# A fused state-space convolution and quantised FFN: down's loads, sums, mask, conversion, bank and skip-term moved

## The reference

```
mask = arange(512) < length[:, None];  u_m = x * mask
K = 2 * real(einsum(Cs, exp(dtA * arange(512))))      # one row of taps per head
y = (causal_conv(u_m, K) + u_m * D) * mask
xq    = int4_quant(y)                                 # scale from mean |y| of the row
w_eff = clip(round(w / mean|w|), -1, 1) * mean|w| * s # for w_gate, w_up, w_down
gate  = relu(xq @ w_gate_eff.T) ** 2;  up = xq @ w_up_eff.T
inter = int8_quant(up * gate)                         # scale from max |.| of the row
out   = x + inter @ w_down_eff.T
```

## Time and profile before

| | us |
|---|---|
| median of three runs | 210.07 |
| the profiled execution | 210.21 |
| its span (first to last instruction) | 208.0 |
| TensorE busy | 176.7 |
| VectorE busy | 166.5 |
| ScalarE busy | 114.2 |
| TensorE idle at 69.67, at 80.68, at 192.34 and at 198.39 | 1.46, 0.96, 0.66, 1.23 |

### The profile page before, as it was taken

How to read it: one execution, slowest core, us unless ns; L and a number is a source line. 1 busy time by engine, 2 the same in 40 slices (tenths; PEclk the granted TensorE clock), 3 DMA queues, 4 the chain that set the end, 5 groups by cost and what they waited for, 6 DMA issues and landing times.

```text
span 208.0 us, 3457 instructions
## 1 busy us (share of the span) xinstructions
PE 176.7 (85%) x1127; PEld 95.1 (46%) x1143; DVE 166.5 (80%) x456; ACT 114.2 (55%) x188; POOL 11.7 (6%) x31
## 2 busy tenths in 40 slices
PE   1011799799999798999999999999999999998973
PEld 1001697555554253455454545444545454543442
DVE  6999778759997686797979788878888787879871
ACT  2277957799817345364554637281919182735630
POOL 5035501100001000000000000000000000000000
PEclk9999999999999999999999999999999999999998
DMA  2999839149999399868596678696786979634524
GB/s 88 378 385 327 287 109 315 66 134 267 204 161 214 76 225 195 209 167 203 130 240 196 153 217 156 130 219 205 147 225 138 230 107 224 171 71 116 117 65 101
DMA packets 50784, 38.31 MB, mean 184 GB/s; under 512 B 37024, under 2 KB 37392, under 8 KB 50768
## 3 DMA queue, kind: packets, MB, share of 16 engines
q1 hardware_dynamic: 49968, 36.57, 71.6%
q10 hardware_dynamic: 416, 1.47, 2.1%
q0 software_dynamic: 384, 0.06, 0.2%
HBM read 25.27 MB, written 4.28 MB: 142 GB/s over the span
## 4 chain that ended last, share of the span: by engine, by line
PE 56%; DVE 16%; DMA 10%; ACT 9%; issue 5%; SPq 3%; DVEq 0%; ACTq 0%
PE down_ps L630 14%; PE conv_ps L500 12%; PE gate_ps L583 12%; PE up_ps L588 10%; DMA it_int<-inter_q 5%; DMA q_int<-y_i 4%; PE tr_act_ps L490 2%; ACT g L739 2%; ACT int_up L669 2%; DVE y L1012 1%; ACT y_i L705 1%; ACT int_gate L682 1%; PE tr_dve_ps L557 1%; ACT int_down L675 1%; DVE inter L1097 1%
## 5 line engine op out<-in xcount | busy, mean ns | idle before, releaser
L697 ACT ACTIVATE y_abs<-y 128x512 bf16<-128x512 f32 x16 | 10.1, 629 | 65.4 <-DVE y L1012 65.4
L588 PE MATMUL up_ps<-up_t,q_t 128*128 128x416 bf16 (+2 forms) x192 | 45.0, 357 | 0.0
L583 PE MATMUL gate_ps<-gate_t,q_t 128*128 128x416 bf16 (+2 forms) x177 | 41.9, 356 | 2.1 <-DVE q_t L1032 1.2
L630 PE MATMUL down_ps<-down_t,i_t 128*128 128x512 bf16 (+1 forms) x164 | 37.9, 379 | 3.8 <-DVE i_t L1138 3.6
L1097 DVE SCALAR_TENSOR_TENSOR inter<-up_ps,gu_scale,g 128x416 f32<-128x416 f32 (+2 forms) x48 | 33.2, 692 | 7.6 <-issue 5.2
L500 PE MATMUL conv_ps<-toep,x_t 128*64 128x512 f32 (+3 forms) x256 | 38.0, 439 | 0.2 <-ACT x_t L693 0.2
L739 ACT ACTIVATE g<-gate_ps,gu_scale 128x416 f32<-128x416 f32 (+2 forms) x48 | 30.3, 631 | 5.0 <-PE gate_ps L583 4.9
L1101 DVE TENSOR_REDUCE imax<-inter 128x1 f32<-128x416 f32 (+2 forms) x48 | 30.3, 631 | 1.6
L742 ACT ACTIVATE g<-g 128x416 f32<-128x416 f32 (+2 forms) x48 | 28.1, 586 | 1.5
L500 PEld LDWEIGHTS conv_ps<-toep,x_t 128*64 128x64 f32 x256 | 17.0, 136 | 23.1 <-issue 20.3
L588 PEld LDWEIGHTS up_ps<-up_t,q_t 128*128 128x128 bf16 x192 | 18.8, 98 | 18.4
(11 more groups left out here) (180 smaller groups left out, 161.6 us busy)
## 6 DMA issues: line engine op xcount, KB each, us to landing
toep<-k_back SPq DMA_DIRECT2D x16, 512.0 KB, 4.9
x_in<-in_x_dram SPq DMA_DIRECT2D x32, 128.0 KB, 3.0
x_res<-in_x_dram SPq DMA_DIRECT2D x32, 128.0 KB, 4.1
out_dram<-o_sb SPq DMA_DIRECT2D x30, 128.0 KB, 2.4
raw_gate<-in_L_ffn_w_gate_dram SPq DMA_DIRECT2D x1, 1536.0 KB, 7.0
raw_up<-in_L_ffn_w_up_dram SPq DMA_DIRECT2D x1, 1536.0 KB, 13.4
raw_down<-in_L_ffn_w_down_dram ACTq DMA_DIRECT2D x1, 1376.0 KB, 7.0
raw_down<-in_L_ffn_w_down_dram SPq DMA_DIRECT2D x1, 1376.0 KB, 8.7
```

Of the source, the lines that this page charges most:

```text
L583: mm = pe.matmul(gate_ps[bank][:, 0:cn], q_t[p][:, i, :], gate_t[:, i, c0:c0 + cn], start=(i == 0), stop=(i == KB - 1))
L588: mm = pe.matmul(up_ps[bank][:, 0:cn], q_t[p][:, i, :], up_t[:, i, c0:c0 + cn], start=(i == 0), stop=(i == KB - 1))
L630: mm = pe.matmul(down_ps[:], i_t[0:r, c, :], down_t[0:r, c, :], start=(c == 0), stop=(c == IB - 1))
```

## The change

Seven edits:

1. **Loads of down.** Both halves of `raw_down` are issued by SP's queue behind the Toeplitz tiles of tiles 0 and 1; the first half was issued by ScalarE's queue after ScalarE's second sum of up. Tile 2's `x` is issued right behind them, ahead of the wait for parts 1 and 2.
2. **Sums.** `down_sum(0)` on VectorE moves from before `y_mask(0)` to behind `q_copy(0)`, where `down_sum(2)` stands.
3. **Taps.** Parts 1 and 2 change places: part 1 is now the first 8 heads of group 1, part 2 the last 12 heads of group 0.
4. **Skip term.** The four loads of `d_tail` are issued by GpSimd ahead of its arithmetic instead of behind it.
5. **x kept.** Six `x` buffers (two of them in the space of `raw_up`) replace two `x_in` and two `x_res`; `add_out` reads the tile that `xt` read, and the 32 loads of `x_res` go. `oscale` gets a third buffer.
6. **Mask and bank.** In iteration 1 `y_mask(3)` goes ahead of `down_copy(0)`. down of tile 0 writes `tr_dve_ps` instead of `down_ps`.
7. **Conversion and output.** In iteration 2 the conversion of `i_t` moves from behind `gated(1)` and `add_out(0)` to ahead of `gated(1)`; `add_out(0)` goes behind `y_mask(4)`. The stores of tiles 0 and 1 are both issued in iteration 3.

```diff
-        x_in = [sb(f"x_in{p}", [P, L]) for p in range(2)]
-        x_res = [sb(f"x_res{p}", [P, L]) for p in range(2)]
+        x_in = [sb(f"x_in{i}", [P, L]) for i in range(4)] + [raw[1][:, i, :] for i in range(2)]
+        NX = len(x_in)
...
-        K_PARTS = [(0, 0, K_EARLY, 0, tr_dve_ps), (0, K_EARLY, HG, 32, tr_dve_ps),
-                   (1, 0, HG // 2, 64, tr_dve_ps), (1, HG // 2, HG, 0, down_ps)]
+        K_PARTS = [(0, 0, K_EARLY, 0, tr_dve_ps), (1, 0, HG // 2, 32, tr_dve_ps),
+                   (0, K_EARLY, HG, 64, tr_dve_ps), (1, HG // 2, HG, 0, down_ps)]
...
             load_toep(1, 1)
-            s = weight_part(2, 1)
-            sp.dma_start(raw[2][s], w_down.rearrange("(c p) i -> p c i", p=P)[s]).then_inc(w_loaded[2][1], 16)
+            for i in range(2):
+                s = weight_part(2, i)
+                sp.dma_start(raw[2][s], w_down.rearrange("(c p) i -> p c i", p=P)[s]).then_inc(w_loaded[2][i], 16)
+            load_x(2)
...
-                elif k >= 2:
-                    sp.wait_ge(out_ready, m - 1)
-                    for half in range(2):
-                        sp.dma_start(in_dram(out, m - 2, half), o_sb[p][half_rows(half), :]).then_inc(stored[p], 16)
+                elif k >= 3:
+                    for n in range(0 if k == 3 else m - 2, m - 1):
+                        sp.wait_ge(out_ready, n + 1)
+                        for half in range(2):
+                            sp.dma_start(in_dram(out, n, half), o_sb[n % 2][half_rows(half), :]
+                                         ).then_inc(stored[n % 2], 16)
...
-                if k is None or k < T:
-                    for half in range(2):
-                        sp.dma_start(x_res[p][half_rows(half), :], in_dram(x, m, half)).then_inc(res_loaded[p], 16)
...
-                wait(pe, out_ready, m - 1)
+                elif k == 2:
+                    pe.wait_ge(k_ready, 4)
+                else:
+                    pe.wait_ge(out_ready, m - 1)
...
-            down_sum(0)
             y_mask(0)
             y_scale(0, 0, step)
             weight_copy(10)
             k_copy(2)
             q_copy(0, 0)
+            down_sum(0)
             down_sum(2)
...
-                if k in (1, 2, T - 1):
+                if k in (1, T - 1):
                     gated(1)
-                if k == 2:
-                    add_out(0, down_ps, slice(0, L), 1)
...
                 if k == 1:
+                    y_mask(3)
                     down_copy(0)
-                    y_mask(3)
                     k_copy(3)
                 if k < T - 2 and k != 1:
                     y_mask(m + 2)
+                if k == 2:
+                    add_out(0, tr_dve_ps, slice(0, L), 1)
```

More of the change, by code:

```diff
@@ L164, in adaln_ffn @@
         iscale = sb("iscale", [P, 1])
-        oscale = [sb(f"oscale{p}", [P, 1]) for p in range(2)]
+        oscale = [sb(f"oscale{i}", [P, 1]) for i in range(3)]
         inter_q = sb("inter_q", [P, IB * P], I16)
@@ L180, in adaln_ffn @@
         w_loaded = [[sem(f"w_loaded{m}{i}") for i in range(3)] for m in range(3)]
-        x_loaded = [sem(f"x_loaded{p}") for p in range(2)]
-        res_loaded = [sem(f"res_loaded{p}") for p in range(2)]
+        x_loaded = [sem(f"x_loaded{i}") for i in range(NX)]
         toep_loaded = [sem(f"toep_loaded{p}") for p in range(2)]
@@ L310, in _, with load_x @@
                 sp.dma_start(dst, src).then_inc(par_loaded, 16)
-            def load_x(tile, p):
+            def load_x(tile):
+                b = tile % NX
+                if tile == 4:
+                    sp.wait_ge(w_rounded[1][0], 1)
                 for half in range(2):
-                    sp.dma_start(x_in[p][half_rows(half), :], in_dram(x, tile, half)).then_inc(x_loaded[p], 16)
+                    sp.dma_start(x_in[b][half_rows(half), :], in_dram(x, tile, half)).then_inc(x_loaded[b], 16)
             def load_inner(m, w):
@@ L326, in _ @@
             load_inner(1, w_up)
-            load_x(0, 0)
-            load_x(1, 1)
+            load_x(0)
+            load_x(1)
             sp.wait_ge(zeros_ready, 1)
@@ L358, in load_ahead @@
                     sp.wait_ge(k_stored[3], 16)
-                sp.wait_ge(xt_turned, n - 1)
-                load_x(n, p)
+                if n > 2:
+                    load_x(n)
                 sp.wait_ge(conv_done, n - 1)
@@ L421, in _ @@
             nc.gpsimd.memset(w_int[2][:, :, I:IB * P], 0).then_inc(pads_ready, 1)
+            pool.wait_ge(zeros_ready, 2)
+            for g, h0, h1, row, bank in K_PARTS:
+                last = row + JA - 1
+                pool.dma_start(d_tail[last:last + 1, h0:h1, JB - 1],
+                               Dskip[g * HG + h0:g * HG + h1].rearrange("(a h) -> a h", a=1),
+                               allow_slow_non_contiguous=True).then_inc(d_loaded, 16)
             steps_done = [0]
@@ L444, in _ @@
             tt(cs[:], cs[:], both(inv_a2[:, 2:3]), ALU.mult).then_inc(cs_ready, 1)
[L446 to L449, removed]
-                               Dskip[g * HG + h0:g * HG + h1].rearrange("(a h) -> a h", a=1),
-                               allow_slow_non_contiguous=True).then_inc(d_loaded, 16)
             pool.wait_ge(w_loaded[1][2], 32)
@@ L486, in xt @@
             def xt(n, j, p):
-                pe.wait_ge(x_loaded[p], 32 * (j + 1))
+                b = n % NX
+                pe.wait_ge(x_loaded[b], 32 * (n // NX + 1))
                 wait(pe, xt_copied, n)
                 for i in range(KB):
-                    mm = pe.transpose(tr_act_ps[:, i * P:(i + 1) * P], x_in[p][:, i * P:(i + 1) * P], ident[:])
+                    mm = pe.transpose(tr_act_ps[:, i * P:(i + 1) * P], x_in[b][:, i * P:(i + 1) * P], ident[:])
                 mm.then_inc(xt_turned, 1)
@@ L626, in down @@
                     pe.wait_ge(down_copied, 2)
-                wait(pe, out_ready, m - 1)
+                elif k == 2:
+                    pe.wait_ge(k_ready, 4)
+                else:
+                    pe.wait_ge(out_ready, m - 1)
                 for c in range(IB):
                     r = P if c < IB - 1 else IR
-                    mm = pe.matmul(down_ps[:], i_t[0:r, c, :], down_t[0:r, c, :],
+                    mm = pe.matmul(down_bank(m - 1)[:], i_t[0:r, c, :], down_t[0:r, c, :],
                                    start=(c == 0), stop=(c == IB - 1))
@@ L643, in body @@
                     if k == 2:
-                        pe.wait_ge(k_ready, 4)
                         down(1, 1)
@@ L1107, in add_out @@
                     dve.wait_ge(down_done, done)
-                    dve.wait_ge(res_loaded[q], 32 * (n // 2 + 1))
+                    dve.wait_ge(x_loaded[n % NX], 32 * (n // NX + 1))
                     wait(dve, stored[q], 32 * (n // 2))
                     v.scalar_tensor_tensor(out=o_sb[q][:, cols], in0=bank[:, 0:cols.stop - cols.start],
-                                           scalar=oscale[q][:], in1=x_res[q][:, cols],
+                                           scalar=oscale[n % 3][:], in1=x_in[n % NX][:, cols],
                                            op0=ALU.mult, op1=ALU.add).then_inc(out_ready, 1)
@@ L1146, in body @@
                         add_out(T - 1, bank, cols, T + h)
-                if k < T - 1 and k not in (1, 2):
+                if k < T - 1 and k != 1:
                     gated(1)
```

6 lines of the change are left out of this document (3 added, 3 removed).

## The result

Four runs of the changed kernel gave 206.90 to 207.23 us, median **207.14 us**; four of the kernel before, run beside them, gave a median of 210.32 us. The ratio is 0.985, with a 95% interval of 0.981 to 0.989: about 3.2 us faster. The profiled execution took 207.19 us with a span of 205.0, so that the two traces differ by 3.0 us.

The account below looks back on a forecast made before the run. TensorE's waits at the start and before down in iterations 2 and 3, behind VectorE and SP's queue, were taken as the places to gain; 0.3 + 1.6 + 1.1 + 0.3 = 3.3 us off 210.07 gives 206.8, range 206.0 to 207.7.

Parts of the forecast that it names:

- the forecast case: Whole launch: 206.8 us on the median's scale, own range 206.0 to 207.7, chance 0.60.
- Iteration 2: TensorE's 1.46 us wait for the conversion before down goes, with the pipe's refilling: 1.6 us, ends nothing and 1.7.
- The 0.15 for the pipe: TensorE in the loop's iteration 2: refilling of the pipe after the wait before down goes, about 0.15 us.
- Mask of tile 3 ahead of `down_copy(0)`: VectorE in iteration 1: same work in another order, worth nothing; at most 0.75 us lost if the copy comes late.
- Iteration 3: q's transposition on SP's queue issued some 5 us earlier, so the conversion's DMA lands in time: 1.1 us.
- Iterations 4 to 15: Loop's rest: 32 loads of 128 KB go, helping only tile 15's wait for q: 0.3 us, ends nothing and 0.66.
- The start: Before the loop's second iteration: what VectorE's list carries on of earlier taps, mask and products: 0.3 us, ends nothing and 0.75.
- Down's loads: SP's queue at the start: second half lands at 41.3 at the latest, wanted at 41.0, costing up to 0.3 us.
- Rival D: Start: down's second half lands far too late, each us after 41.0 costing one; 210.8 us, reaching 213; chance 0.04.
- Rival A: Start gives gain back: slow TensorE rate past conv(0), or late tap store delaying conv(2) 1.5 us; 208.3 or 207.3; chance 0.15.
- Rival B: One wait stays before down in iteration 2 or 3, 1.1 to 1.6 us missing: 207.9 to 208.4; chance 0.09.
- the rule of turns between the queues: DMA engines alternate packets between queues, so GpSimd's part 2 tap store would pass the backlog and its 1.5 us price vanish.

Follow-up runs that it names:

- The start's part alone: Kernel before with only edits 1 to 4 (loads of down, sums, taps, skip term), its loop as before; 209.69 us, ratio 0.999.
- Conversion back: Changed kernel with the conversion of iteration 2 behind `gated(1)` again, `add_out(0)` still behind the mask of tile 4; 206.75 us, ratio 0.985.
- conversion and mask back: Changed kernel with iteration 2's conversion behind `gated(1)` again and the mask of tile 3 behind `down_copy(0)` again; 208.30 us, ratio 0.994.

## Why the prediction was right, and where it was not

207.14 us against the forecast 206.8, inside its range, and faster as the forecast case said. Its steps:

- *Iteration 2*, 1.6 booked, 1.83 measured: right, but 0.13 above its upper end of 1.7, which took the extra down at its whole 2.55 us; it stretched the iteration by only 12.25 - 9.87 = 2.38. The 0.15 for the pipe is borne out: a down that had not waited started 0.16 us before the recorded end of the matmuls ahead of it (68.11 against 67.35 + 0.92). Within the term the causes were put wrong. "Mask of tile 3 ahead of `down_copy(0)`" was booked at nothing and the conversion's own move taken as the cause. Conversion back costs 0.06 us, conversion and mask back 1.07, so that with the mask early the conversion's own move was worth nothing, and the mask's place was worth 1 us once the conversion was late.
- *Iteration 3*, 1.1 booked, 1.13 measured: right, and its cause, q's place behind the stores, is shown for 0.74 of it by the run that puts them back. For q of tile 4, behind four stores, VectorE waited 0.76 us at 81.20 and TensorE not at all; with the same four stores that wait was 0.22 to 0.38 us or none in the other runs, so the stores are not shown to be its cause.
- *Iterations 4 to 15*, 0.3 booked at tile 15's q: the size came, the place did not. Products of tile 15 still wait 0.69 us. The 0.32 is one interval of 10.19 us in the kernel before's execution (134.81 to 145.00), in which the conversion at 139.63 had waited 0.76 us for its DMA and down started only behind it, at 140.22. The start's part alone keeps the 32 loads of `x_res` and shows no such interval, so the loads that went need not be its cause; I take it for chance in one execution, which was not tested, and the agreement with the 0.3 booked for luck.
- *The start*, 0.3 booked with ends nothing and 0.75, -0.25 measured: **the step that failed**, and below its lower end. Not in TensorE's part (products of tile 0 came 2.31 us earlier, where 0.65 was booked; in the other executions with the start's edits and no recorded fall of the clock they came at 38.75 to 39.64, 0.46 to 1.35 us earlier, so that a good part of the 2.31 is the clock and not the edits), but in "Down's loads". The text set the landing at "41.3 at the latest" and the cost at 0.3 at most. The second half landed at 41.6 here, and at 40.9 to 42.2 in the other runs that move both halves. Three things were mis-sized. The rates were means of full stretches and left out the end, where the rate falls from 416 to 169 and 44 GB/s while the sum waits for the last byte. "ScalarE's issue that goes overlapped a sum, and costs nothing" looked at the issue and not at its bytes: the load that had filled idle DMA time at 397 GB/s went into the full stretch, and with it back on ScalarE's queue the second half needs 10.6 us to its landing instead of 13.6. And the lower end of nothing held only if the landing was early enough: with the landing in charge each us that the other edits save at the start is given back as a wait, so the term was never 0.75 minus something, but 60.38 minus (landing + 19.0). Smaller: the two sums were dated from 39.37, where the 40.07 of now less the 0.65 booked gives 39.42.
- Rival D, whose price was each us of landing after 41.0, was thus at work in small: 60.0 was forecast, 60.63 came, with the landing 0.6 after 41.0. Its condition for a launch slower than before, past 44.3, was far away.
- Rival A: the `toep` wait at conv(2) did not come. The 24 KB store was issued at 37.57 and landed 4.7 us later, at 42.3, where 44.8 had been feared. Its other branch, the slow rate, went the other way in this execution. Rival B did not come either: no wait stayed before down. How small stores fare beside the backlog is better seen at part 1's, 16 KB, issued at 30.02. The DMA issues of 28 to 33 us:

```profile
raw_down<-in_L_ffn_w_down_dram SPq DMA_DIRECT2D x1, 1376.0 KB, 13.6
x_in<-in_x_dram SPq DMA_DIRECT2D x2, 128.0 KB, 12.3
k_back<-k_sb POOLq DMA_DIRECT2D x1, 16.0 KB, 5.7
```

The second half of down and tile 2's `x`, issued before it on SP's queue, landed near 41; it landed at 35.7 and passed them. So far the rule of turns between the queues (the Trainium skill, DMA: Bandwidth & Descriptors, Queues, rings and completion order) agrees with the trace; the price did not fall away with it, as 5.7 us is what the store of before took.

That the sum was right within 0.3 us rests on the loop's two terms, which were read from waits of TensorE in plain view. For the rest it is in part luck: the start's miss of 0.55 was offset by 0.23 more in iteration 2, and the 0.3 booked for the end came from another place.

## What to carry to other kernels

A load that is moved behind others is to be dated at its last byte, and held against the time at which its user will want it after the other edits, not before them; from that point on it swallows every us that they save. A load that is taken out of a stretch in which DMA has nothing else to do is not free, even if nobody waits for it there. A wait with several delays ahead of it does not belong to any one of them: undo each alone and together before crediting one. On an in-order queue, what stands behind a store inherits the wait of that store, and taking it out is worth looking for first.

## What the runs showed of the hardware

**The granted clock.** The changed kernel's execution records it falling at the start, while TensorE is busy without a gap; it had last been idle for 1.78 us up to 25.13 (columns as in the earlier trace rows):

```profile
25.00:26.00 1.00, 0.87 (x8) 0.70 (x9) 1.00 (x4) 1.00 (x2) 0.08 (x1) 1.00 0.10 9
...
27.00:28.00 1.00, 1.00 (x16) 0.91 (x14) 1.00 (x1) 1.00 (x2) 0.00 (x0) 0.50 0.35 45
...
30.00:30.60 0.60, 0.60 (x12) 0.50 (x10) 0.35 (x1) 0.60 (x2) 0.56 (x1) 1.00 1.08 256
```

The level goes from 1.00 (2.4 GHz) to 0.50 (1.2 GHz) between 26 and 27 us and back between 29 and 30. One other execution, that with mask and conversion back, recorded such a fall. In both there had been the full rate before it: part 0's 16 passes at 22.62 took 0.73 us in the first, against 1.03 in all others, and part 1's 32 at 26.00 took 1.11 us in the second, against 1.89 in the kernels of the same order that recorded no fall. Their conv(0) began at 31.15 and 31.51. The other eight executions read 1.00 from 24 to 33 us, while their passes took 57 to 64 ns up to 29, against 33 to 35 ns later, and their conv(0) began at 32.1 to 34.0. The same twelve transposes took 1.38 us at 28.34 in the changed kernel, where the record says 0.50, and 1.38 at 30.11 in the kernel before, where it says 1.00; twelve like them at full rate took 0.78 in both. So the record does not show every stretch at half rate, and the moment at which the full rate comes differs between executions of nearly the same work, by up to some 2 us. The Trainium skill (TensorE: Matmul & The Clock Gate, What's actually happening) says that the release comes at a moment that differs from run to run; the ten traces agree. It moves one execution against another at conv(0), so that the start of a single profile can't be compared with that of another without a look at these passes.

**Landing of a large load.** The two loads of 1376 KB, issued one after the other from 27.48 on behind two Toeplitz tiles, moved at 416 GB/s from 33 to 39 us; yet the second was complete 13.6 us after its own issue. From the first issue to the last landing it took 13.97 to 14.35 us in five executions.

**A small store beside a large load.** What moves that issue is the store of part 0's taps (8 KB, SP's queue), on which the Toeplitz tiles wait. In the five kernels that load nothing beside it, it took 1.6 to 2.7 us; in the five whose first half of down is on ScalarE's queue at that time, 3.2 to 4.2 us.
